# Collecting a gated projection by pairs of row tiles in a long-convolution block on one core

## What is computed

```python
xp = (einsum('btd,de->bte', X, Wp) + bp).reshape(B, T, 4, D)   # the projection and its bias
f  = (pos @ Wf + bf).reshape(T, 3, D)                          # the filters
y  = xp[:, :, 0, :]
for i in range(3):
    y = causal_conv(y, f[:, i]) * xp[:, :, i + 1, :]
x = layernorm(X + y)
x = layernorm(x + down(silu(gate(x)) * up(x)))
```

## Time and profile before

| | |
|---|---|
| median of three runs | 778.7 us (778.18 to 779.78) |
| profiled execution | 777.92 us |
| its span, first to last instruction | 776.1 us |
| TensorE's mean granted clock | 0.998 |
| TensorE matmul busy | 743.4 us (96%) |
| VectorE busy | 553.9 us (71%), 1098 instructions |
| ScalarE busy | 489.0 us (63%) |
| GpSimd busy | 419.2 us (54%) |
| shares of the chain that ended last | PE 90%, DVE 3%, DMA 2%, POOL 2% |

### The profile page before, as it was taken

One profiled execution on the slowest core, in us unless ns is written; L12 is line 12 of the kernel. 1 busy time (PEld: TensorE's weight loads), 2 busy tenths in 40 slices (PEclk: granted clock), 3 DMA queues, 4 the chain that ended last, 5 costly groups with the idle time before them and its releaser, 6 DMA issues.

```text
span 776.1 us, 16249 instructions
## 1 busy us (share of the span) xinstructions
PE 743.4 (96%) x6056; PEld 560.6 (72%) x6056; DVE 553.9 (71%) x1098; ACT 489.0 (63%) x976; POOL 419.2 (54%) x483
## 2 busy tenths in 40 slices
PE   6999999999999999999999998889999999999996
PEld 5878877888788888888888886546565666566663
DVE  4897777777888888888888887655565566565544
ACT  3454554443477888878886664355677766677744
POOL 3445535544243444434444345686777777877553
PEclk9999999999999999999999999999999999999999
DMA  8659757999998999998999997111111231110101
GB/s 302 207 186 322 254 189 266 316 309 328 296 273 247 262 259 258 257 258 250 249 270 280 277 319 220 35 56 54 55 55 55 66 98 57 55 54 29 54 30 54
DMA packets 161997, 144.84 MB, mean 187 GB/s; under 512 B 4096, under 2 KB 145536, under 8 KB 161664
## 3 DMA queue, kind: packets, MB, share of 16 engines
q1 hardware_dynamic: 160064, 138.50, 58.9%
q10 hardware_dynamic: 1856, 5.31, 2.1%
HBM read 109.45 MB, written 34.34 MB: 185 GB/s over the span
## 4 chain that ended last, share of the span: by engine, by line
PE 90%; DVE 3%; DMA 2%; POOL 2%; issue 1%; ACT 1%; POOLq 0%; DVEq 0%; ACTq 0%
PE bank L374 22%; PE bank L446 20%; PE bank L428 19%; PE bank L467 10%; PE bank L387 8%; PE bank L408 3%; PE bank L409 3%; PE bank L410 3%; PE bank L438 2%; DMA toep<-filter_rows 2%; DVE prod L790 2%; POOL x L233 1%; PE bank L483 1%; ACT yl L587 1%; DMA xt<-in_XT 1%
## 5 line engine op out<-in xcount | busy, mean ns | idle before, releaser
L978 POOL TENSOR_TENSOR y<-y,gate 128x512 f32<-128x512 f32 (+1 forms) x108 | 124.4, 1156 | 174.8 <-DVE y L815 163.0
L374 PE MATMUL bank<-wps,xs 128*128 128x512 f32 x768 | 183.0, 398 | 10.1 <-DVE wps L748 6.7
L428 PE MATMUL bank<-prod,ei 128*128 128x256 f32 x720 | 186.1, 381 | 0.0
L374 PEld LDWEIGHTS bank<-wps,xs 128*128 128x128 f32 x768 | 144.8, 190 | 42.4 <-POOL xs L1005 11.4
L790 DVE TENSOR_TENSOR prod<-bank,wfx 128x512 f32<-128x512 f32 x180 | 124.1, 690 | 41.5 <-PE bank L387 41.5
L1005 POOL TENSOR_TENSOR xs<-xt,xs 128x256 fp32r<-128x256 f32 x128 | 92.8, 741 | 104.2 <-ACT xs L577 103.8
L446 PE MATMUL bank<-xh,wq 128*128 128x512 f16 x384 | 145.6, 379 | 2.0 <-DVE hf L856 1.6
L446 PE MATMUL bank<-xl,wq 128*128 128x512 f16 x384 | 145.5, 379 | 0.0
L997 POOL TENSOR_TENSOR hl<-hf,hh 128x512 f16<-128x512 f32 x95 | 109.0, 1156 | 54.2 <-ACT hh L634 54.0
L856 DVE SCALAR_TENSOR_TENSOR hf<-bank,sg 128x512 f32<-128x512 f32 x96 | 64.3, 684 | 94.0 <-ACT sg L630 48.0
L428 PEld LDWEIGHTS bank<-prod,ei 128*128 128x128 f32 x720 | 122.8, 190 | 11.5
(11 more groups left out here) (78 smaller groups left out, 1252.4 us busy)
## 6 DMA issues: line engine op xcount, KB each, us to landing
toep<-filter_rows SPq DMA_DIRECT2D x43, 1024.0 KB, 7.8
gate<-gates SPq DMA_DIRECT2D x48, 512.0 KB, 3.8
xt<-in_XT SPq DMA_DIRECT2D x31, 512.0 KB, 5.4
gates<-st SPq DMA_DIRECT2D x24, 512.0 KB, 4.2
gates<-toep SPq DMA_DIRECT2D x24, 512.0 KB, 3.9
xr<-in_X SPq DMA_DIRECT2D x16, 512.0 KB, 4.8
out_x<-oo SPq DMA_DIRECT2D x15, 512.0 KB, 3.2
toep<-filter_rows SPq DMA_DIRECT2D x10, 512.0 KB, 6.9
```

Of the source, the lines that this page charges most:

```text
L374: mm = pe.matmul(b_proj[n % PBK][:, :], xs[:, n % XSS, hx, k, :], wps[:, hw, k, p * 512:(p + 1) * 512], start=(k == 0 and q == 0), stop=(k ...
L428: mm = pe.matmul(b_out[m % 2][:, half * W:(half + 1) * W], ei[:, h, e0 * P:(e0 + 1) * P], prod[:, n % 3, h, :], start=(h == 0), stop=(h == 1))
L978: nc.gpsimd.tensor_tensor(y[:, u % NG, a:a + count, :], y[:, u % NG, a:a + count, :], gate[:, a:a + count, :], ALU.mult).then_inc(gated, 1)
```

## The change

`collect` is called for odd n only and takes row tiles n - 1 and n together. The eight banks become one PSUM tensor, so that one operation can read two neighbouring banks (2 and 3, or 4 and 5). For each channel it reads the element of the first bank and then that of the second, adds the bias, which is read twice by a broadcast, and writes the two results to neighbouring addresses: two batches of the innermost index, 8 bytes of every 16. `proj_used` is counted up by 2.

```diff
-        bank = [ctx.enter_context(nc.psum_tensor(f"bank{i}", [P, 512], F32)) for i in range(8)]
+        psum = ctx.enter_context(nc.psum_tensor("bank", [P, 8, 512], F32))
+        bank = [psum[:, i] for i in range(8)]
...
                 def collect(n):
-                    p, m, b = n // NT, n // NB, n % NB
+                    p, m, h = n // NT, n // NB, n % NB // 2
                     s, a = m % 2, m % NA
-                    src = b_proj[n % PBK]
-                    if b == 0 and m >= 2:
+                    src = psum[:, 2 + 2 * h:4 + 2 * h]
+                    bs = slice(2 * h, 2 * h + 2)
+                    if h == 0 and m >= 2:
                         dve.wait_ge(g_out[s], staged(m - 2) if m - 2 < NA else NA // 2 * 16 + ((m - 2 - NA) // 2 + 1) * 32)
                     dve.wait_ge(proj_done, n + 1)
                     if p == 0:
                         nc.vector.tensor_tensor(
-                            y[:, :, a, :].rearrange("p g (c b) -> p g c b", b=NB)[:, :, :, b],
-                            src[:, 0:D].rearrange("p (g c) -> p g c", g=NG),
-                            bp[:, 0:D].rearrange("p (g c) -> p g c", g=NG), ALU.add)
+                            y[:, :, a, :].rearrange("p g (c b) -> p g c b", b=NB)[:, :, :, bs],
+                            src[:, :, 0:D].rearrange("p b (g c) -> p g c b", g=NG),
+                            bp[:, 0:D].rearrange("p (g c) -> p g c", g=NG).unsqueeze(3).broadcast_to([P, NG, CG, 2]), ALU.add)
                         nc.vector.tensor_tensor(
-                            st[s][:, 0].rearrange("p g (c b) -> p (g c) b", b=NB)[:, :, b],
-                            src[:, D:2 * D], bp[:, D:2 * D], ALU.add).then_inc(proj_used, 1)
+                            st[s][:, 0].rearrange("p g (c b) -> p (g c) b", b=NB)[:, :, bs],
+                            src[:, :, D:2 * D].rearrange("p b e -> p e b"),
+                            bp[:, D:2 * D].unsqueeze(2).broadcast_to([P, D, 2]), ALU.add).then_inc(proj_used, 2)
                     else:
                         nc.vector.tensor_tensor(
-                            st[s].rearrange("p s g (c b) -> p (s g c) b", b=NB)[:, :, b],
-                            src[:, :], bp[:, 2 * D:4 * D], ALU.add).then_inc(proj_used, 1)
+                            st[s].rearrange("p s g (c b) -> p (s g c) b", b=NB)[:, :, bs],
+                            src.rearrange("p b e -> p e b"),
+                            bp[:, 2 * D:4 * D].unsqueeze(2).broadcast_to([P, 2 * D, 2]), ALU.add).then_inc(proj_used, 2)
...
-                    collect(n)
+                    if n % 2:
+                        collect(n)
...
-                    collect(NT + n)
+                    if n % 2:
+                        collect(NT + n)
```

## The result

The changed kernel takes 780.76 us (median of 13 runs, 779.22 to 784.14) against 778.63 us for the kernel before (13 runs): a ratio of 1.0032, 95% interval 1.002 to 1.0044. A second comparison, with 12 and 29 runs, gave 780.22 against 778.42 us, 1.0022 (1.0012 to 1.0032). So the change costs 0.2 to 0.3%. The forecast of 779.2 us was 1.6 us low; the measured time lies in the whole range, but above the 780.1 us at which the likeliest case's own range ends, and beyond the 0.2% that was called "no change". The profiled execution took 779.78 us, 1.9 more than that of before.

A forecast was written before the change was run, and what follows sets the result against it. TensorE was taken as the bound, the change acting only through its four projection stops; 0 + 0 + 0.22 + 0.15 + 0.15 = +0.5 us, put on the 778.7 us median, gave 779.2 us, range 777.7 to 784.3.

The forecast's parts named there:

- the likeliest case: The forecast itself, operations at 0.69 and 1.21 us: 779.2 us, own range 778.0 to 780.1, chance 0.48.
- TensorE's four places: Projection stops, TensorE resuming at 47.21, 109.08, 117.57 and 203.38 us: 4.8 us in all, a collect on each path.
- part 1: VectorE's pair operations, reading two banks in turn, take 0.69 us for 512 elements and 1.21 for 1024.
- Parts 2, 3 and 6: Later collect start, sine rows around 23 us, store and low-part order: 0 us each; waits for stores should go.
- Part 4 (coefficients): Coefficient operations around the pair (16, 17): TensorE idles 1.1 us near 46 us, as before, so 0.
- Part 5 (the three ends): Last collect of pass one, collect ahead of the scale factors, last collect of all: +0.22, +0.15, +0.15 us.
- rival A: The alternating read costs 1.80 ns an element, like the scattered write: +4.7 us, 783.4 us, chance 0.38.

The follow-up runs named there:

- Single collects: Changed kernel with row tiles 62, 63, 68, 69, 126 and 127 collected one by one as before: 779.19 us, 1.0013 against the kernel before.
- spread groups: Changed kernel with the three coefficient groups behind pairs (14, 15), (16, 17) and (18, 19): 777.73 us, 0.9987 against the kernel before.
- one-bank-then-the-other kernel: Changed kernel with each pair operation going through one bank, then the other, writing single elements: 790.39 us, 1.014 against the kernel before.

## Why the prediction was right or wrong

**What bounds the kernel** was right: TensorE's four places are where the change adds its idling, and each is held by a collect. Single collects shortened three of them and spread groups removed the other. That the change can act on the end only through them was not the whole of it, as the clock shows.

**The price of an operation** (part 1), on which the verdict was said to hang, was right at its lower end: 0.69 and 1.23 us against 0.69 and 1.21. The reason given for choosing it, that the scattered write makes the difference, is what the one-bank-then-the-other kernel shows.

**Parts 2, 3 and 6** were right as to time: no stop in the steady stretches and none near 28 us. The waits for stores mostly went, and it didn't matter. (There were three of them before, not four: 1.15 us and two like it.)

**Part 4 (coefficients)** said 0 and measured +0.24 us. In the timeline the pair (16, 17) starts 0.11 us behind the end of the matmul it waits for, where I took none; it takes 1.21 us to the next start where I took 1.15, and the two groups take 4.09 where I took 4.04. These three are the 0.2 us.

**Part 5 (the three ends)** said 0.22, 0.15 and 0.15; measured 0.21, 0.31 and 0.32. The first was right. The other two were sized by operation times (1.21 less 1.06), but what counts is when the next operation on VectorE starts: behind the collect at 113.51 us the next one began 0.91 us later, and in the changed kernel 1.14 us after 115.25:

```profile
115.25 1.22 DVE L770 TENSOR_TENSOR toep<-bank,bp 128x1024 f32<-128x1024 f32 x1 [1.55 <-PE bank L375]
116.39 0.16 DVE L777 TENSOR_REDUCE total<-bank 128x1 f32<-128x8 f32 x1
```

The slow operations overlapped their successor by 0.15 us, the new ones by 0.08; I took 0.14 for all. The collect also begins later behind the end of its matmuls, by 0.10 us at the third place and 0.06 at the fourth. The pair at the third place opens a staging tile, and so has two semaphores to wait for, where tile 69's collect had one. That is not all of it: through the second pass, wherever VectorE waited for matmuls, pairs begin 0.14 us behind them if they open a staging tile and 0.11 if they don't, while row tiles begin 0.11 or 0.04 us behind. Why a pair takes longer to begin is open.

**The sum** was thus 0.5 us where the places measure 1.1. **What was missing** is the clock, which falls in more executions of the changed kernel, an estimated 0.6 us on the average. No part of the prediction had it, and the first profiled executions of the two kernels don't show it, for neither has a fall. That it is the longer stop at the fourth place which lets it fall more often is argued and not shown: pairs in the second pass alone (stop of 1.69 us, fallen in 9 of 12) and in the first alone (1.38 us, 2 of 12) speak for it, pairs with spread groups (1.69 us, 1 of 12) against it. The clock also makes rival A's time far too low: 4.7 us there, some 12 in the kernel that has A's prices. The chances (0.48 same, 0.45 slower) were put on the price of the read alone. With the price known to be low the change still came out slower, by way of terms that were all called small. The range held the result by luck: the likeliest case, whose price came true, ended at 780.1 us, and only rival A, whose price did not, carried the range to 784.3.

## What to carry to other kernels

Work that is hidden need gain nothing by being made cheaper: here 54 us of VectorE time went and nothing came of it. Look at the few places where the bound engine stops, ask what is queued behind what there, and move that; here a dozen operations in another order were worth more than a faster form of 192. And when a stage's granule is doubled, count the places where its last piece is on the path: there the price of a whole granule counts, less what of it used to be hidden.

## What the runs showed of the hardware

VectorE reads two PSUM banks element by element in turn at the rate at which it reads one (692 ns for 512 elements against 690 for an operation that reads one bank; 1226 ns for 1024), and reads the other source twice by a broadcast without loss. Writing single 4-byte elements 16 bytes apart costs 1.8 ns each (623, 1083 and 2014 ns for 256, 512 and 1024 elements), and runs of two in the same 16 bytes 1.04 ns.

TensorE's clock fell from 2.4 to 1.2 GHz for 3.4 us behind stops of 1.37, 1.69, 1.91, 2.14, 2.34 and 2.66 us, between long stretches at 2.4 GHz, and one such fall cost 1.05 to 1.6 us. It stayed up behind stops of 1.37, 1.69 and 2.09 us in other profiles or at other places, so in some executions and not in others of the same kernel; and the kernel with spread coefficient groups had the 1.69 us stop and read 0.997 or more in 11 of 12. What besides the stop decides it is open.
